# Three stages of a Perceiver forward pass: a score bank handled by ScalarE and GpSimd, a new order on TensorE, a cast on ScalarE

## The reference, cut to what matters

```python
def _L1_attn_ref(X, Wq, bq, Wk, bk, Wv, bv, Wo, bo):     # 32 query heads of width 8, 8 key heads
    scores = jnp.einsum('bkgqd,bkld->bkgql', q, k) * scale
    weights = jax.nn.softmax(scores, axis=-1)
    out = jnp.einsum('bkgql,bkld->bkgqd', weights, v)
    return out.reshape(b, s, N_HEAD * HEAD_DIM) @ Wo.T + bo

def _L2_attn_ref(...):                                   # time mixing
    x = _layer_norm(hidden_state, ln_w, ln_b)            # norm of the norm of x
    sx = shifted x;  xk, xv, xr = sx + mix * (x - sx)
    r = sigmoid(xr @ Wr.T);  k = xk @ Wk.T;  v = xv @ Wv.T
    out = residual + (r * wkv(k, v, time_decay)) @ Wo.T  # residual: the norm of x; x adds it once more

def _L2_ffn_ref(x, w_gating, w_linear):                  # operands rounded to float8, results bfloat16
    activations = gelu(qdot(x, w_gating[0])) * qdot(x, w_gating[1])
    return qdot(activations, w_linear)
```

## Time and profile before

| | us |
|---|---|
| median of 3 runs | 3065.69 (3065.61 to 3072.91) |
| profiled execution | 3077.68 |
| its span, first to last instruction | 3075.9 |
| TensorE busy (matmuls) | 2728.7 (89%) |
| VectorE busy | 1893.7 (62%) |
| ScalarE busy | 1383.5 (45%) |
| GpSimd busy | 1025.0 (33%) |
| self attention, core loop | 1121 to 1247 |
| time mixing, last three chunks | about 1822 to 1931 |
| feed forward (float8) | 1932 to 2039 |

### The profile page before, as it was taken

The page is one execution under the profiler, slowest core; times in us unless marked ns, Lnnn a source line. Parts: engine busy times, 40 slices in busy tenths (PEclk is TensorE's granted clock), DMA queues, the critical chain, the costliest instruction groups (busy, mean ns, idle before and its releaser), DMA issues. The chain is left out here.

```text
span 3075.9 us, 51163 instructions
## 1 busy us (share of the span) xinstructions
PE 2728.7 (89%) x19364; PEld 1712.7 (56%) x19364; DVE 1893.7 (62%) x2524; ACT 1383.5 (45%) x2652; POOL 1025.0 (33%) x868
## 2 busy tenths in 40 slices
PE   7999987999989888889989875678988898899899
PEld 5999953466646647433346532235643555554687
DVE  3666646222268737334468688768854899996433
ACT  3333344121256646222257554546667666653123
POOL 1222200133135422000036400015610899991462
PEclk9999999999999999999999987889999999999999
DMA  4000005111200000200000000000010111213124
GB/s 157 21 27 20 17 7 182 57 45 45 76 23 2 23 1 2 86 1 0 9 14 2 15 0 0 0 22 2 2 42 37 59 69 71 81 47 113 61 88 148
DMA packets 77016, 128.94 MB, mean 42 GB/s; under 512 B 12112, under 2 KB 54736, under 8 KB 76304
## 3 DMA queue, kind: packets, MB, share of 16 engines
q1 hardware_dynamic: 67888, 101.78, 9.9%
q0 software_dynamic: 8928, 24.39, 2.5%
HBM read 107.40 MB, written 18.74 MB: 41 GB/s over the span
## 5 line engine op out<-in xcount | busy, mean ns | idle before, releaser
L3456 POOL TENSOR_TENSOR h<-ssm_u,ss_bc 128x1024 f32<-128x1024 f32 x88 | 205.8, 2359 | 0.0
L3419 ACT ACTIVATE ssm_p_h<-ss_delta,ss_decay 128x256 f32<-128x256 f32 x352 | 146.6, 464 | 125.2 <-DVE ctxT L3493 84.1
L3366 PE MATMUL ssm_p_y<-ctxT,ident 128*128 128x512 f32 x412 | 187.6, 595 | 0.0
L684 POOL TENSOR_TENSOR xw_prob<-xw_prob,xw_rsum 128x512 f32<-128x512 f32 x64 | 65.2, 1039 | 259.2 <-DVE xw_rsum L633 259.2
L3488 DVE TENSOR_TENSOR_SCAN ssm_p_h<-ssm_p_h,h 128x1024 f32<-128x1024 f32 x64 | 145.8, 2279 | 8.6 <-ACT ssm_p_h L3419 6.8
L3446 POOL TENSOR_TENSOR ctxT<-ctxT,ss_bc 128x1024 f32<-128x1024 f32 x50 | 117.5, 2359 | 20.1 <-DVE ctxT L3486 20.1
L3366 PEld LDWEIGHTS ssm_p_y<-ctxT,ident 128*128 128x128 f32 x412 | 76.5, 192 | 79.6 <-issue 78.5
L515 PE MATMUL xw_p_q<-h,xw_m_h 128*128 (+1 forms) x1024 | 119.3, 278 | 1.3 <-PEq L60 1.3
L515 PEld LDWEIGHTS xw_p_q<-h,xw_m_h 128*128 128x128 f32 x1024 | 116.3, 193 | 7.0 <-issue 7.0
L3350 PE MATMUL ssm_p_h<-ssm_b_diagonal,ssm_uT 128*128 128x128 f32 x640 | 83.7, 286 | 39.7 <-DVE ctxT L3493 20.1
L523 PE MATMUL xw_p_q<-xw_u,xw_vo_h 128*128 128x128 f32 x1024 | 117.1, 275 | 1.2 <-ACT xw_u L587 1.2
(11 more groups left out here) (868 smaller groups left out, 7147.5 us busy)
## 6 DMA issues: line engine op xcount, KB each, us to landing
ss_bc<-ss_bc_rows SPq DMA_DIRECT2D x24, 896.0 KB, 4.3
xw_ctx_rows<-in_ctx_rows SPq DMA_DIRECT2D x32, 256.0 KB, 2.6
ss_bc<-ss_bc_rows SPq DMA_DIRECT2D x8, 768.0 KB, 4.1
L3f_rows<-L3f_rows_out SPq DMA_DIRECT2D x16, 384.0 KB, 4.0
L0f_wg<-in_L_ffn_gate SPq DMA_DIRECT2D x9, 512.0 KB, 9.7
L0f_wu<-in_L_ffn_up SPq DMA_DIRECT2D x9, 512.0 KB, 9.7
L0f_wd<-in_L_ffn_down SPq DMA_DIRECT2D x9, 512.0 KB, 9.7
L0f_rows<-L0f_rows_out SPq DMA_DIRECT2D x16, 256.0 KB, 4.0
```

What stands on the lines that cost most here:

```text
L684: g.tensor_tensor(prob[:, n % 2, part, :], prob[:, n % 2, part, :], bcast(rsum[:, 1, part], 2, S2), ALU.mult).then_inc(sem["normed"], 1)
L3366: mm = pe.matmul(p_y[:, 2 * half:2 * half + 2, :].rearrange("p e t -> p (e t)"), k.ident[:, :], weighed[n % RING_W][:, ts(half, CH)], star ...
L3419: i = act.activation(out[:, ts(e, CT)], delta[:, e, ts(c, CT)], ACT.Exp, scale=decay[:, E4 * s + e:E4 * s + e + 1])
L3456: g.tensor_tensor(tiles(drive[n % RING]), u[:, c % 2, :, :], bcast(bcs[:, row_b(s), :], 1, E4), ALU.mult).then_inc(sem["driven_g"], 1)
```

## The change

Self attention: bank 3 of the scores is copied to SBUF (`raw`) by ScalarE, right after the exponential of the tile before. VectorE takes maxima over banks 0 to 2 from PSUM and over raw from SBUF, and subtracts in banks 0 to 2; GpSimd subtracts in raw. nmax has two buffers. The exponential waits for both subtractions, and the next scores for the subtraction on VectorE and the copy on ScalarE. The two last tiles are written out on ScalarE and GpSimd, and so are the two first on GpSimd.

Time mixing: the residual part of `project_out` becomes `residual(c)`; the last chunk's output goes to p_p in place of p_y. Mean 0 and mean 1 of `following` stand between residual and projection of chunks 1 and 2, variance 0 ahead of the projections of chunk 3, variance 1 ahead of the last output projection, followed by six calls of keep_warm.

Feed forward: the cast moves from VectorE to ScalarE, ahead of pairs 7, 11 and 15 and at the end; VectorE's additions follow pairs 7, 11 and 15 and the end.

```diff
@@ self attention
-            nmax = sb(k, mid, "nmax", [P, 4, 8])
+            raw = sb(k, mid, "raw", [P, 4, 2, S])
+            nmax = sb(k, mid, "nmax", [P, 2, 4, 8])
@@ score(i)
                         pe.wait_ge(sem["shifted"], i)
+                        pe.wait_ge(sem["copied"], i)
@@ scalar
+                def copy_raw(i, free=True):
+                    act.wait_ge(sem["scored"], i + 1)
+                    if free:
+                        act.wait_ge(sem["moved"], i)
+                    act.copy(raw[:, :, :, :], p_s[:, 3, :, :, :]).then_inc(sem["copied"], 1)
...
                     act.wait_ge(sem["shifted"], i + 1)
+                    act.wait_ge(sem["moved"], i + 1)
                     act.activation(prob[:, u, :, :, :, :], prob[:, u, :, :, :, :], ACT.Exp, scale=scale).then_inc(sem["exped"], 1)
+                    if not last:
+                        copy_raw(i + 1)
@@ vector
-                    v.tensor_reduce(nmax[:, :, :], p_s[:, :, :, :, :]..., negate=True).then_inc(sem["maxed"], 1)
+                    v.tensor_reduce(nmax[:, u, 0:3, :], p_s[:, 0:3, :, :, :]..., negate=True)
+                    v.wait_ge(sem["copied"], i + 1)
+                    v.tensor_reduce(nmax[:, u, 3, :], raw[:, :, :, :]..., negate=True).then_inc(sem["maxed"], 1)
...
-                    v.tensor_tensor(prob[:, u, :, :, :, :]..., p_s[:, :, :, :, :]...,
+                    v.tensor_tensor(prob[:, u, 0:3, :, :, :]..., p_s[:, 0:3, :, :, :]...,
@@ gpsimd
+                def move(i, u, free=True):
+                    g.wait_ge(sem["copied"], i + 1)
+                    g.wait_ge(sem["maxed"], i + 1)
+                    if free:
+                        g.wait_ge(sem["turned"], 4 * i - 4)
+                    g.tensor_tensor(prob[:, u, 3, :, :, :]..., raw[:, :, :, :]...,
+                                    bcast(nmax[:, u, 3, :], 2, S), ALU.add).then_inc(sem["moved"], 1)
...
-                        g.wait_ge(sem["scored"], 2 * j + u - 1)
-                        spread_q(2 * j + u, u)
+                        move(2 * j + u, u)
+                        spread_q(2 * j + u + 2, u)
@@ time mixing
+        outs = [p_y] * (NCH - 1) + [p_p]
...
-            def project_out(c):
-                if c >= 1:
+            def residual(c):
+                if c == NCH - 1:
+                    pe.wait_ge(sem["kept"], H2 * 3 * NCH)
+                elif c >= 1:
                     pe.wait_ge(sem["added"], c)
...
             for c in range(NCH):
-                if c >= 2:
-                    follow_mean(c - 2)
                 if c + 2 < NCH:
                     ln1.var(pe, c + 2)
+                if c == 2:
+                    follow_var(0)
                 if c + 1 < NCH:
                     for n in range(3):
                         project(c + 1, n)
-                if c >= 2:
-                    follow_var(c - 2)
...
+                residual(c)
+                if 1 <= c < 3:
+                    follow_mean(c - 1)
+                if c == 3:
+                    follow_var(1)
+                    keep_warm(pe, k, ln2.p_mean[:, 0, :], 6)
                 project_out(c)
@@ feed forward, scalar
+            def unload(c):
+                act.wait_ge(sem["out"], PAIRS * c + PAIRS)
+                if c >= 1:
+                    act.wait_ge(sem["residual"], c)
+                act.copy(yb[:, :, :], outs[c % 2][:, :, :]).then_inc(sem["unloaded"], 1)
...
+                if m % 2 == 0 and n > LAG + 1 and (n - LAG - 2) % PAIRS == PAIRS - 1:
+                    unload((n - LAG - 2) // PAIRS)
...
+            unload(NCH - 1)
@@ vector
-            def unload(c):
-                v.wait_ge(sem["out"], PAIRS * c + PAIRS)
-                if c >= 1:
-                    v.wait_ge(sem["residual"], c)
-                v.tensor_copy(yb[:, :, :], outs[c % 2][:, :, :]).then_inc(sem["unloaded"], 1)
+            def add(c):
                 v.wait_ge(sem["unloaded"], c + 1)
                 v.tensor_tensor(k.x[:, :, ts(c, CH)], k.x[:, :, ts(c, CH)], yb[:, :, :], ALU.add).then_inc(sem["residual"], 1)
...
-                if n >= LAG and (n - LAG) % PAIRS == PAIRS - 1:
-                    unload(n // PAIRS - 1 if n < NP else NCH - 1)
+                if n >= LAG + 2 and (n - LAG - 2) % PAIRS == PAIRS - 1:
+                    add((n - LAG - 2) // PAIRS)
+            add(NCH - 1)
```

More of the change, by code:

```diff
@@ L2025, in self_attention @@
         with ExitStack() as mid:
-            sem = semaphores(nc, mid, k.prefix, "q_spread scored maxed shifted exped turned turned_read mixed mixed_read returned recip weighed")
+            sem = semaphores(nc, mid, k.prefix, "q_spread scored copied maxed shifted moved exped turned turned_read mixed mixed_read returned recip weighed")
             qx = sb(k, mid, "qx", [P, 2, H2, 2, 4, S])
             prob = sb(k, mid, "prob", [P, 2, 4, 4, 2, S])
+            raw = sb(k, mid, "raw", [P, 4, 2, S])
             probT = sb(k, mid, "probT", [P, 4, 4, P])
             oT = sb(k, mid, "oT", [P, 4, P])
-            nmax = sb(k, mid, "nmax", [P, 4, 8])
+            nmax = sb(k, mid, "nmax", [P, 2, 4, 8])
             rsum = sb(k, mid, "rsum", [P, 4, 4, 2])
@@ L2095, in _, with tile @@
                 act.preload_act_table(ACT.Exp)
-                def tile(i, u):
+                def copy_raw(i, free=True):
[3 more added lines that the diff above has]
+                    act.copy(raw[:, :, :, :], p_s[:, 3, :, :, :]).then_inc(sem["copied"], 1)
+                def tile(i, u, last=False):
                     act.wait_ge(sem["shifted"], i + 1)
+                    act.wait_ge(sem["moved"], i + 1)
                     act.activation(prob[:, u, :, :, :, :], prob[:, u, :, :, :, :], ACT.Exp, scale=scale).then_inc(sem["exped"], 1)
+                    if not last:
+                        copy_raw(i + 1)
                     for m in range(4):
@@ L2104, in tile @@
                     act.copy(oT[:, :, :], p_m[:, :, :]).then_inc(sem["mixed_read"], 1)
-                with act.Fori(0, NT // 2) as j:
+                copy_raw(0, free=False)
+                with act.Fori(0, NT // 2 - 1) as j:
                     for u in range(2):
                         tile(2 * j + u, u)
+                tile(NT - 2, 0)
+                tile(NT - 1, 1, last=True)
             @block.vector
@@ L2117, in soft @@
                         v.wait_ge(sem["turned"], 4 * i - 4)
-                    v.tensor_tensor(prob[:, u, :, :, :, :].rearrange("p r m b s -> p (r m b) s"), p_s[:, :, :, :, :].rearrange("p r m b s -> p (r m b) s"),
-                                    bcast(nmax[:, :, :].rearrange("p r m -> p (r m)"), 2, S), ALU.add).then_inc(sem["shifted"], 1)
+                    v.tensor_tensor(prob[:, u, 0:3, :, :, :].rearrange("p r m b s -> p (r m b) s"), p_s[:, 0:3, :, :, :].rearrange("p r m b s -> p (r m b) s"),
+                                    bcast(nmax[:, u, 0:3, :].rearrange("p r m -> p (r m)"), 2, S), ALU.add).then_inc(sem["shifted"], 1)
                 def weigh(i):
@@ L2145, in spread_q @@
                     last.then_inc(sem["q_spread"], 1)
+                def move(i, u, free=True):
+                    g.wait_ge(sem["copied"], i + 1)
+                    g.wait_ge(sem["maxed"], i + 1)
+                    if free:
+                        g.wait_ge(sem["turned"], 4 * i - 4)
+                    g.tensor_tensor(prob[:, u, 3, :, :, :].rearrange("p m b s -> p (m b) s"), raw[:, :, :, :].rearrange("p m b s -> p (m b) s"),
+                                    bcast(nmax[:, u, 3, :], 2, S), ALU.add).then_inc(sem["moved"], 1)
                 spread_q(0, 0)
                 spread_q(1, 1)
-                with g.Fori(1, NT // 2) as j:
+                for u in range(2):
+                    move(u, u, free=False)
+                    spread_q(2 + u, u)
+                with g.Fori(1, NT // 2 - 1) as j:
                     for u in range(2):
-                        g.wait_ge(sem["scored"], 2 * j + u - 1)
-                        spread_q(2 * j + u, u)
+                        move(2 * j + u, u)
+                        spread_q(2 * j + u + 2, u)
+                move(NT - 2, 0)
+                move(NT - 1, 1)
         k.prefix = "sao_"
@@ L2586, in project_out @@
                     for a in range(H2):
-                        mm = pe.matmul(p_y[:, o, :], w[:, 3, a, ts(o, P)], fo[:, c % 2, a, :], start=False, stop=a == H2 - 1, skip_group_check=True)
+                        mm = pe.matmul(outs[c][:, o, :], w[:, 3, a, ts(o, P)], fo[:, c % 2, a, :], start=False, stop=a == H2 - 1, skip_group_check=True)
                 mm.then_inc(sem["out"], 1)
@@ L2738, in add @@
                 v.wait_ge(sem["out"], c + 1)
-                v.tensor_tensor(k.x[:, :, ts(c, CH)], k.x[:, :, ts(c, CH)], p_y[:, :, :], ALU.add).then_inc(sem["added"], 1)
+                v.tensor_tensor(k.x[:, :, ts(c, CH)], k.x[:, :, ts(c, CH)], outs[c][:, :, :], ALU.add).then_inc(sem["added"], 1)
             ln1.centre(v, 0)
```

7 lines of the change are left out of this document (5 added, 2 removed).

## The result

The changed kernel took 3050.56 us in the median of 4 runs (3049.32 to 3053.68), the kernel before 3069.11 beside it (3065.61 to 3072.91): ratio 0.9934 with a 95% interval of 0.9922 to 0.9947. Timed again, in more runs on one chip, it took 3046.15 against 3070.34, ratio 0.9921 (0.9907 to 0.9935). Forecast were 3042.2, in a range of 3036 to 3053, and a saving of 23.5 us. The two ratios amount to 20 and 24 us. The profiled execution took 3051.77, its span is 3050.0. Two executions in the comparisons of single edits further down, 9525 us of the kernel before and 3931 us with the feed forward edit alone, count as slow and stand in no ratio.

The account below looks back on a forecast made before the run. Three edited stages, bound mostly by VectorE's work and waits, lie in series; self attention 6.0, time mixing 10.5 and feed forward 7.0 sum to 23.5 us, from 3065.7 to 3042.2, range 3036 to 3053.

Parts of the forecast that it names:

- Stages in series, savings come off whole: All three edited stages: each ends in a barrier of all engines, so savings shorten the span fully, 23.5 us together.
- the ring: Self attention: VectorE's cycle per tile, from scores through maximum and subtraction to the next scores, 6.93 us becoming 6.48.
- upper bound of 7.3: Self attention: the most that the edit was expected to save, in us, beside 6.0 taken and a lower bound of 2.
- ScalarE's ring: Self attention: ScalarE's cycle per tile, exponential through copies to the next exponential, 6.64 us less 0.1 to 0.2.
- 0.9 for tiles at the lower clock: Self attention: us deducted because tiles with TensorE at its lower clock find no slack on ScalarE; bounds none and two.
- Rival A: Self attention: ScalarE's or GpSimd's cycle takes over, the tile stays at 6.9; 17.5 us saved, 3048.2; chance 0.13.
- rival C: Self attention: GpSimd's subtraction delays every exponential; from 1.6 us late the tile exceeds 6.93, possibly 3079 in all; chance 0.08.
- Points 1 to 4: Time mixing: waits before first centring (3.4 us), scaling (2.8) and second centring (3.0) go; variance of chunk 1 costs nothing.
- Point 5: Time mixing, end: last residual done early, 8 records remain; wait 4.7 us against 6.05, 1.3 saved, bounds -1.1 and 2.4.
- 3.75 and 1.15: Feed forward: us saved by three casts leaving VectorE's unbroken run, and by the third addition falling behind the last pair.
- B: Time mixing and feed forward: TensorE's new order, last projection's lower clock or gelu waits give time back; 17 saved, 3048.7; chance 0.13.
- Signs: Profile after: maxima 6.5 apart, named waits gone, under 5 us at time mixing's last addition, gelu idles at most 0.5.

Follow-up runs that it names:

- first pair of profiles: Kernel before and changed kernel, one profiled execution each, all three edits between them: spans 3075.9 and 3050.0 us.
- second pair: Kernel before and changed kernel, both unchanged, each profiled once more: spans 3067.8 and 3045.2 us.

## Why the prediction was right, and where its steps were off

*Stages in series, savings come off whole.* Right within the noise: single edits of 4.6, 8.6 and 7.1 against 20 and 24 for all three. One carry-over was not foreseen: in the profile of the time mixing edit the feed forward is 1.7 us shorter too.

*Self attention.* Right in every duration but the copy's (0.59 for 0.54), and the ring was worked out as 6.48 where 6.45 was measured. The value taken, 6.0 us, was too small: the stage is 7.1 to 8.7 shorter. In the first pair of profiles it is even beyond the upper bound of 7.3. Two things were mis-sized. I had ScalarE's ring level with VectorE's and took 6.50; by the doubled copy it has nearly 0.4 of slack. And I took off 0.9 for tiles at the lower clock, but all 15 periods after are 6.41 to 6.51. The price of such a tile was well guessed, though: the one that came, with the subtraction on VectorE, took 0.9 us more (7.33). Rival A is out with the periods, and rival C by the doubled subtraction.

*Time mixing.* Points 1 to 4 right in the first pair of profiles: 3.44 at the first centring (3.4 forecast), the waits before the scaling and the second centring gone, VectorE 9.4 us ahead at the last product (9.2). That the numbers meet so closely is in part luck, since both profiles have the same waits early in the stage; in the second profile of the kernel before, the wait at the first centring was 1.49, and no more than that can be saved there. Point 5 is the term that was wrong: 1.3 saved was forecast, 0.8 lost was measured in the first profile, within the bounds given (-1.1 to 2.4), and 0.4 saved in the second pair (5.38 against 5.79). The residual is out of the way, yet the projection does not run at the higher clock throughout: the warming ends 3.5 us before it, 4.9 to 5.2 in the other profiles; with ten calls and a pause of 1.6 it does. I had read the lower clock after an idle of 3.89 and then still taken 4.7 from between the two levels. The stage takes 178.2 to 179.7 us in the four profiles without the edit and 168.9 to 172.3 in the six with exactly this time mixing: 8.9 less on average, 8.6 in the first pair; forecast were 10.5.

*Feed forward.* Right: 6.9 in the first pair of profiles, 7.1 by the single edit, 7.0 forecast. In the profile of the single edit the stage is 6.6 shorter: four casts of 1.22 are off VectorE, 4.9 us (forecast 3.75 and 1.15), and its idle times over 0.3 us sum to 10.7 instead of 12.4, 1.7 less (1.85). With all three edits one of the two gelu waits came back, as the 1.27 before pair 14. What made up for it was not in the prediction: VectorE waits 0.92 before pair 1 (2.14 before). This wait is 2.01 to 2.14 in the four profiles without the time mixing edit and 0.57 to 0.93 in the ten with it or a variant of it, where the variance at the start of the stage (4 records on TensorE) takes 2.41 to 3.27 instead of 3.62.

*Total.* 23.5 forecast, 20 and 24 measured. That it fits so well is partly two errors that cancel: in the first pair of profiles self attention saved 2.7 more than forecast and time mixing 1.9 less. The 18.5 between the first medians was a small sample: before's 4 runs lay in two pairs at 3065.6 and 3072.7. The time itself, 3042.2, was 8.4 and 4.0 too low; the kernel before, with medians of 3069.1 and 3070.3, lay 3.4 and 4.6 above the 3065.7 that I subtracted from. The ratios alone do not shut out rivals A and B (17.5 and 17 saved): the first leaves 16.3 to 23.9 us, only the second, 20.0 to 28.6, excludes them. The stages do: of B one part of three came true, the last projection at the lower clock.

*Signs.* Those of self attention held, and so did those of the waits before the centrings and the scaling. Two did not: 6.85 at the last addition, where under 5 was named, and 1.27 for the gelu, where 0.5 was. That no other stage should change by over 1 us was no usable sign, since the rest differs by 5.6 between two profiles of the kernel before.

## What to carry to other kernels

When engines hand one buffer round in a ring, look for the part of the work that must end before the buffer is free, and move only that out of the ring. Which engine gets the rest matters little, as long as its other waits leave room; test that by doubling one engine's part, since an instruction that starts without idle time doesn't show that its engine is the bound. And look where a warming burst ends: here it gave the higher clock throughout only where it reached to within 1.6 us of the work that it was for, and that even this shortens the kernel is not shown.
